# The end of an FP4 feed-forward stage: where tile 28's down product stands on TensorE, and which engine scales tile 31 up

## The reference

```python
def fp4_quant_dequant(x):
    xb = x.reshape(shape[:-1] + (shape[-1] // BLOCK, BLOCK))
    scale = jnp.max(jnp.abs(xb), axis=-1, keepdims=True) / 6.0
    scale = jnp.maximum(scale, jnp.float32(1e-12))
    xn = xb / scale
    idx = jnp.searchsorted(_MID, jnp.abs(xn))
    q = _GRID[idx] * jnp.sign(xn) * scale
    return q.reshape(shape)
def fp4_linear(x, w):
    return jnp.einsum('bsk,nk->bsn', fp4_quant_dequant(x), fp4_quant_dequant(w))
gate = fp4_linear(x, w_gate)
y = fp4_linear(x, w_up)
h = jax.nn.silu(gate) * y
return fp4_linear(h, w_down)
```

## Time and profile before

| what | value |
| --- | --- |
| runs | 919.53 us median of 3 (919.25 to 924.06) |
| the profiled execution's own time | 917.53 us |
| its span, first to last instruction | 915.7 us |
| TensorE busy | 882.7 us (96%) |
| VectorE busy | 779.6 us (85%) |
| ScalarE busy | 522.3 us (57%) |
| GpSimd busy | 458.9 us (50%) |
| mean granted TensorE clock | 0.998 |
| last instruction of the span ends | VectorE's residual of tile 31, 912.99 + 0.42 us, then its store |

### The profile page before, as it was taken

How to read it: one execution, slowest core, us unless ns; L and a number is a source line. 1 busy time by engine, 2 the same in 40 slices (tenths; PEclk the granted TensorE clock), 3 DMA queues, 4 the chain that set the end, 5 groups by cost and what they waited for, 6 DMA issues and landing times.

```text
span 915.7 us, 20182 instructions
## 1 busy us (share of the span) xinstructions
PE 882.7 (96%) x7216; PEld 794.8 (87%) x7216; DVE 779.6 (85%) x2117; ACT 522.3 (57%) x1147; POOL 458.9 (50%) x661
## 2 busy tenths in 40 slices
PE   7899999999899999999899999999979999999998
PEld 5799999998799999998899999999868888888886
DVE  6999999999767777766799999999878898989886
ACT  3534343434588888887465656565644444444543
POOL 2233433433476667654224343334257777777771
PEclk9999999999999999999999999999999999999999
DMA  9120000000000000001000000000000000000001
GB/s 330 74 105 2 2 2 1 2 2 1 2 1 1 1 1 1 1 2 56 1 2 2 1 2 2 1 3 2 1 1 1 24 24 24 0 24 24 24 2 46
DMA packets 6515, 18.31 MB, mean 20 GB/s; under 512 B 912, under 2 KB 3344, under 8 KB 5904
## 3 DMA queue, kind: packets, MB, share of 16 engines
q1 hardware_dynamic: 5552, 16.65, 4.8%
q10 hardware_dynamic: 864, 0.37, 0.2%
HBM read 12.83 MB, written 4.19 MB: 19 GB/s over the span
## 4 chain that ended last, share of the span: by engine, by line
PE 72%; DVE 10%; ACT 9%; POOL 6%; issue 3%; POOLq 0%; DVEq 0%; ACTq 0%
PE a_psO L1232 14%; PE s_psY L1450 10%; PE s_psH L1439 9%; PE f_psGU L1945 7%; PE a_psQ L1194 6%; PE a_psT L1221 6%; PE a_psS L1173 5%; PE f_psY L1937 5%; ACT a_qTs L1118 4%; ACT a_prob L1101 3%; POOL f_hval L1774 2%; PE a_psQ L1182 2%; POOL f_hres L1780 2%; PE a_psY L1182 1%; DVE f_hid L1611 1%
## 5 line engine op out<-in xcount | busy, mean ns | idle before, releaser
L1232 PE MATMUL a_psO<-vblk,a_prob 128*128 128x51 f32 (+1 forms) x1280 | 148.4, 271 | 0.0
L1232 PEld LDWEIGHTS a_psO<-vblk,a_prob 128*128 128x128 f32 x1280 | 148.0, 192 | 0.0
L1945 PE MATMUL f_psGU<-late_wgu,f_xTs 128*128 128x512 f32 (+1 forms) x576 | 139.8, 387 | 2.7 <-ACT f_silu L1856 2.7
L950 DVE TENSOR_REDUCE a_mx<-a_psS 128x4 f32<-128x308 f32 x256 | 115.3, 471 | 9.7 <-PE a_psS L1173 4.3
L1945 PEld LDWEIGHTS f_psGU<-late_wgu,f_xTs 128*128 128x128 f32 x576 | 103.2, 191 | 17.4 <-DVE f_xTs L1590 3.0
L1101 ACT ACTIVATE a_prob<-a_psT 128x512 f32<-128x512 f32 (+1 forms) x192 | 101.8, 530 | 23.0 <-PE a_psT L1221 21.9
L1089 ACT COPY a_xTs<-a_psQ 128x256 f32<-128x256 f32 x64 | 23.9, 373 | 159.4 <-PE a_psQ L1182 159.2
L958 DVE TENSOR_TENSOR a_shifted<-a_psS,a_mx 128x308 f32<-128x308 f32 x256 | 114.7, 469 | 0.0
L1221 PE MATMUL a_psT<-ident,a_shifted 128*128 128x128 f32 x640 | 105.3, 279 | 8.3 <-ACT a_prob L1101 5.0
L1450 PEld LDWEIGHTS s_psY<-e_w,s_hid 128*128 128x128 f32 x768 | 100.1, 188 | 8.8 <-POOL s_hid L1370 3.6
L1058 POOL TENSOR_TENSOR a_rstd<-a_mv,expo 128x1 f32<-128x1 f32 x64 | 15.1, 237 | 182.8 <-DVE a_mv L988 182.8
(11 more groups left out here) (193 smaller groups left out, 1829.5 us busy)
## 6 DMA issues: line engine op xcount, KB each, us to landing
out_x<-x SPq DMA_DIRECT2D x7, 512.0 KB, 2.6
x<-in_x SPq DMA_DIRECT2D x3, 1024.0 KB, 16.0
w<-in_w SPq DMA_DIRECT2D x1, 2304.0 KB, 8.5
w<-in_w SPq DMA_DIRECT2D x2, 1024.0 KB, 13.4
a_mask<-in_mask SPq DMA_DIRECT2D x4, 308.0 KB, 3.7
wat<-in_att SPq DMA_DIRECT2D x1, 1024.0 KB, 16.3
x<-in_x SPq DMA_DIRECT2D x1, 768.0 KB, 10.1
wat<-in_att SPq DMA_DIRECT2D x2, 256.0 KB, 4.5
```

The costliest lines, as they stand in the source:

```text
L950: nc.vector.tensor_reduce(mx[:, u, j * BH:(j + 1) * BH], psS[j][:, 0:BH * KV].rearrange("p (h k) -> p h k", k=KV), AX.X, ALU.max).then_inc ...
L1232: mm = nc.tensor.matmul(psO[:, CH[c] * VW:(CH[c] + n) * VW], prob[:, u, c * P:(c + 1) * P], vblk[:, t // R, c * NJ * VW:(c * NJ + n) * VW] ...
L1945: mm = nc.tensor.matmul(psGU[:, n0:n1], xTs[:, u, a, k * P:(k + 1) * P], wgu[:, b, k, n0:n1], start=(n == 0), stop=(n == len(TERMS) - 1))
```

## The change

Four edits, all for the end of the FP4 layer:

1. TensorE, step 31: the down product of tile 28 moves from between segment 0 and segment 1 of tile 31's gates to behind segment 2.
2. Tile 31's scaling up moves from VectorE (two parts) to GpSimd (`h_up`, one instruction of 704 columns), and the lowering of the inverse from VectorE to ScalarE (`h_lowered`). VectorE's `last_exponents` waits for `hval_ready` instead of its own count. GpSimd then waits for both parts of tile 31's exponents before it scales tile 30 down.
3. VectorE's rounding of tile 30 moves from ahead of tile 31's hidden to behind tile 31's inverse. Its `last_down` of the first part also waits for tile 30's `hres_ready`, which keeps the count in order.
4. ScalarE: `h_lowered` of tile 31 stands first in `last_tile`, and the copies of tile 30 move behind the two kicks of tile 31.

```diff
--- before.py
+++ after.py
@@ -1637,15 +1637,9 @@
             nc.vector.tensor_tensor(self.groups[n][1][1], self.banks[n % 4][:, 0:self.groups[n][2]],
                                     self.groups[n][1][0].bitcast(F32), ALU.subtract).then_inc(w_low, 1)
 
-        def last_up(t, u, part, lowered_set):
+        def last_exponents(t, u, part):
             lo, hi = LAST_PARTS[part]
-            dve.wait_ge(dve_own, lowered_set)
-            return kept(nc.vector.tensor_tensor(blocks(hval[:, u, lo:hi]), blocks(hid[:, u, lo:hi]),
-                                                spread(hinv[:, u, lo // QB:hi // QB], (hi - lo) // QB), ALU.mult))
-
-        def last_exponents(t, u, part, up_set):
-            lo, hi = LAST_PARTS[part]
-            dve.wait_ge(dve_own, up_set)
+            wait(dve, hval_ready, t + 1)
             if part == 0:
                 wait(dve, kick_ready, t - 1)
             nc.vector.tensor_scalar(hpow[:, u, lo:hi].bitcast(I32), hval[:, u, lo:hi].bitcast(I32), 0x7F800000,
@@ -1665,24 +1659,20 @@
             dve.wait_ge(dve_own, rounded_set)
             if part == 0:
                 wait(dve, self.hT_mm, 2 * t - 2)
+                wait(dve, hres_ready, t)
             nc.vector.tensor_tensor(blocks(hres[:, u, lo:hi]), blocks(hval[:, u, lo:hi]),
                                     spread(ham[:, u, lo // QB:hi // QB], (hi - lo) // QB), ALU.mult
                                     ).then_inc(hres_ready, 1)
 
         def last_tile():
             t, u = T - 1, (T - 1) % 2
-            h_rounded(t - 1, 1 - u)
             hidden(t, u)
             ham_set = h_largest(t, u)
             hscale_set = h_scale(u, ham_set)
-            dve.wait_ge(dve_own, hscale_set)
-            inverse_set = kept(nc.vector.reciprocal(hinv[:, u, :], ham[:, u, :]))
-            dve.wait_ge(dve_own, inverse_set)
-            lowered_set = kept(nc.vector.tensor_scalar(hinv[:, u, :], hinv[:, u, :], 1.0 - 2.0 ** -22, None, ALU.mult))
-            up_sets = [last_up(t, u, 0, lowered_set)]
-            up_sets.append(last_up(t, u, 1, lowered_set))
-            last_exponents(t, u, 0, up_sets[0])
-            last_exponents(t, u, 1, up_sets[1])
+            h_inverse(u, hscale_set)
+            h_rounded(t - 1, 1 - u)
+            last_exponents(t, u, 0)
+            last_exponents(t, u, 1)
             residual(t - 2)
             rounded_set = last_rounded(t, u, 0)
             last_down(t, u, 0, rounded_set)
@@ -1799,6 +1789,9 @@
                     deviations((i + 6) // SG)
                 wait(pool, hexp_set, min(i + 1, T))
                 wait(pool, xpow_ready, min(i + 4, T))
+            if i == T - 1:
+                h_up(i, i % 2)
+                wait(pool, hexp_set, T + 1)
             if valid(i - 1) and i < T:
                 h_down(i - 1, (i - 1) % 2)
             if valid(i + 3):
@@ -1877,11 +1870,13 @@
 
         def last_tile():
             t, u = T - 1, (T - 1) % 2
-            for n in (t - 2, t - 1):
-                hT_copies(n, n % 2)
-                hT_rest(n, n % 2)
+            h_lowered(t, u)
+            hT_copies(t - 2, u)
+            hT_rest(t - 2, u)
             last_kick(t, u, 0)
             last_kick(t, u, 1)
+            hT_copies(t - 1, 1 - u)
+            hT_rest(t - 1, 1 - u)
             hT_copies(t, u)
             hT_rest(t, u)
 
@@ -1964,7 +1959,7 @@
                 wait(pe, xT_low, i + 1)
                 wait(pe, silu_ready, i)
                 products(u, 0)
-            if valid(i - 3):
+            if valid(i - 3) and i != T - 1:
                 down_product(i - 3, 1 - u, 0, NF1 // 2 if i == T else NF1)
             if valid(i + 1):
                 wait(pe, xres_ready, i + 2)
@@ -1978,6 +1973,8 @@
                 wait(pe, hid_ready, i)
                 products(u, 1).then_inc(gu_mm, 1)
                 products(u, 2).then_inc(gu_mm, 1)
+            if i == T - 1:
+                down_product(i - 3, 1 - u, 0, NF1)
             if i == T + 1:
                 last_transposes(0)
                 last_transposes(1)
```

## The result

| | before | changed |
| --- | --- | --- |
| median of 15 runs | 921.46 us | 926.28 us |
| lowest and highest | 918.16, 926.49 | 922.0, 928.2 |
| ratio of the runs | | 1.0049, 95% interval 1.0035 to 1.0064 |
| span of the profiled execution | 915.7 | 925.5 |
| its mean granted TensorE clock | 0.998 | 0.989 |

The change costs about 4.5 us, 3.2 to 5.9 by the interval: half a per cent. The two profiled executions differ by 9.8 us in span, and more than half of that has nothing to do with the change: tile 30's hidden starts at 899.98 instead of 894.23 us, although nothing ahead of it was altered (a second profile of the unaltered kernel, further down, has it at 899.36). From here on I compare the **tail**: from the start of tile 30's hidden to the end of the last residual.

What follows compares the result with a forecast made beforehand. TensorE was taken to bound the kernel, busy 96% of the span, with its end a chain of latencies across queues. Terms 1 to 3 (+4.04) plus clock (+0.70) on the 919.53 median gave 924.3 us, range 922.3 to 926.0.

Steps and rivals of the forecast that it cites:

- Terms 1 to 3: Kernel's end: tile 31's hidden and scaling up, and tile 30's late scaling down holding tile 29's residual; together +4.04 us.
- term 2: Tile 31's scaling up on GpSimd: a longer series, exponents at 905.90 instead of 905.32, +0.58 us.
- Term 4: TensorE's clock near the end: falls to half after idle time, +0.7 us, between 0 and +1.7.
- a full clock throughout: Sign against the forecast: no clock below 1.00 in the windows from 905 to 911, which points to rival A.
- rival A: TensorE's clock at the end holds or falls where it costs nothing: +4.04, 923.6 us; chance 0.30.
- B: Kernel's end: tile 30's lateness is hidden, only tile 31's series counts: +0.58, 920.1 us; chance 0.06 together with D.
- C: TensorE's lower clock lies wholly over the path: +1.7 instead of 0.7, giving +5.7, 925.3 us; chance 0.09.
- D: Real gain: tile 31's hidden starts at 900.7 and nothing waits for tile 30, 919.2 us; chance 0.06 together with B.

Runs made afterwards that it cites:

- e3: Changed kernel with the residual of tile 28 moved behind tile 31's exponents; tail 24.11 us, ratio to before 1.0043.
- e5: Changed kernel without GpSimd's wait for both parts of tile 31's exponents ahead of tile 30's scaling down; tail 22.51 us, ratio to before 1.0044.
- e4: Changed kernel with tile 29's down product issued whole, ahead of tile 30's transposes; tail 22.50 us, ratio to before 1.0031.
- e9: Kernel before with tile 31 scaled up on GpSimd, lowering on ScalarE behind tile 29's copies, tile 30's copies ahead of the kicks; tail 19.83 us, ratio 0.9989.
- e2: Changed kernel with tile 30's rounding back ahead of tile 31's hidden and tile 30 scaled down before tile 31 is scaled up; tail 25.05 us, ratio to before 1.0052.
- e6: Kernel before with tile 31's scaling up on GpSimd and lowering on ScalarE, in the changed ScalarE order; tail 23.50 us, ratio 1.003.
- e8: As e6, but ScalarE copies tile 29 before lowering tile 31's inverse; tail 22.89 us, ratio to the kernel before 1.005.
- e1: Changed kernel with tile 28's down product back between segments 0 and 1 of tile 31's gates; tail 22.92 us, ratio to before 1.0047.
- e7: Kernel before with tile 31's gates ahead of product 28, its silu and hidden earlier, residuals 28 and 29 later; tail 18.77 us, ratio 0.9989.

## Why the prediction was right

**Terms 1 to 3 came out as worked.** Times from tile 30's hidden (894.23 in the forecast, 899.98 measured): hidden of tile 31 at 7.39 forecast, 7.37 measured; exponents 11.67 and 11.64; tile 30's scaling down 12.34 and 12.32; its transposes 13.77 and 13.76; tile 29's residual 15.98 and 15.96; rounding 16.31 and 16.30; tail +4.04 and +4.02. Each link has an experiment that loosens it: e3 takes the residual of tile 28 away (hidden 0.97 earlier), e5 the wait for the exponents (0.7), e4 the hold on product 29 (the rounding 2.1 earlier), and e9 leaves term 2 alone (0.65).

**Term 4 was too large here.** I took +0.7 for the clock from the one stretch near 677 us. The mechanism exists: four of the experiments show it in their tails, and there it cost 1.6 to 1.8 us, my upper end of 1.7 (by the time from the start of product 29 to that of product 30, 3.33 in e9: 4.89 in e2, 5.01 in e3, 5.00 in e6; in e8 by product 30). But in both profiles of the changed kernel it did not occur, and filling the gaps gave nothing that can be measured. By the sign that I had set myself, "a full clock throughout, which makes it A", these two executions are rival A's. How often the clock falls in the tail of the changed kernel stays open: the two profiles count for little more than one, since their earlier falls stand at the same places too (to 0.1 us, the last at 683.8 and 683.9), and e6, with 3.41 us without work, did fall. The rule of the Trainium skill ("TensorE: Matmul & The Clock Gate", "HAM oscillation"), that only longer gaps need be avoided, which I set aside, would have given the tail of these two profiles; the fall in e8, after 2.20 us without work, speaks against it.

**The time itself.** 926.28 was measured where I wrote 924.3, and it lies 0.3 above my range of 922.3 to 926.0; but before's median over 15 runs is 921.46, not the 919.53 of three on which I built, and the range was meant as a difference of +2.8 to +6.5. As a difference it is +4.5 by the ratio, +3.45 (3.1 to 3.8) at equal clock, +4.02 by the tails, and +4.74 in my forecast. The second comparison of the same kernel gave only +1.8 (none to +3.9), and all 27 runs of it have a mean 3.8 us (2.8 to 4.7) above the unaltered kernel's 109. The forecast is nearest to the first ratio, the sum without term 4, 4.04, to all the others. So that +4.74 met the first comparison so closely is in part luck: its last 0.7 is a fall that the profile of that comparison does not have. That the fit at equal clock is half a microsecond below the tails is not explained; the mean clock has three digits and also counts stretches that cost nothing.

**The rivals.** B needed tile 30's lateness to be hidden; the wait of 3.73 shows that it was not. Its price for the scaling up alone, 0.58, was right (e9: 0.65). C's 1.7 is the size of a fall, not its mean. D: e3 has hidden 6.4 after tile 30's and still a tail far above before's.

**What I overlooked.** I wrote that ScalarE's new order costs nothing. In the changed kernel this is so by the rows: product 29's first half is done 1.25 us before the transposes of tile 30 can start. No run has the changed kernel with ScalarE's old order alone. By itself the new order costs 1.6 by the working (e6 against e9 as expected), 21.8 - 19.8 = 2.0 by the tails without the fall, and at equal clock 2.3 - 0.5 = 1.8 us (with 0.7 to each side): a third cause, hidden behind the second. Loosening one link alone (e1 to e5) does not bring the time back; e9, which undoes all but tile 31's scaling up and lowering, does.

## What to carry to other kernels

Making a result ready earlier is worth nothing while the consumer's queue holds another wait in front: follow each moved instruction to the next wait on every engine, and ask what is queued behind that wait. At the end of a kernel, moving work to an idle engine lengthens the series by what the slower instruction and the hand-overs take more (0.65 us here, e9), and there is nothing behind it to hide that. Where runs of one kernel spread by more than the effect, compare a fixed stretch of the trace, and the times at equal granted clock; the latter understate a change that lowers the clock itself.

## What was unexpected of the hardware

The spread of a kernel's times goes mostly with TensorE's clock. With the same program, before's executions had a mean granted clock from 0.987 to 1.0 and times from 917.1 to 926.9 us. The changed kernel's profile (0.989) and before's second (0.991) show stretches at 0.5 near 11, 236, 458 and 683 us, the changed kernel's one near 32 besides; before's first (0.998) shows one alone, near 679.

A VectorE exponent instruction beside a GpSimd multiply took three times as long (1.82 against 0.60 for two), while its rounding, with one operand in PSUM, did not slow down and slowed nothing (0.83 and 0.89 beside GpSimd's 1.39 in every step). A VectorE instruction of only 44 columns took 0.37 beside GpSimd in e7 and 0.20 with GpSimd idle.
